# A new order, a third bank for the maxima and unread products for TensorE in a four-layer transformer kernel

## The reference: what is computed

```python
x = _layernorm(x + _L0_attn_ref(x, ...))   # causal attention with rotary positions, 16 heads of 16 features
x = _layernorm(x + _L0_ffn_ref(x, ...))    # 8 experts, each token goes to its best one; 256 -> 512 -> 256, gelu
x = _layernorm(x + _L1_attn_ref(x, ...))   # local attention (window 128) mixed with 64 pooled latent tokens
x = _layernorm(x + _L1_ffn_ref(x, ...))    # 8 experts, one per sequence; 256 -> 64 -> 256, relu
```

## Time and profile before

| | |
|---|---|
| Median of three runs | 1435.85 us |
| The profiled execution | 1435.74 us |
| its span, first to last instruction | 1433.9 us |
| mean granted TensorE clock | 0.943 of full speed |
| PE, DVE, ACT, POOL busy | 84%, 65%, 42%, 19% |

### The profile page before, as it was taken

The page is one execution under the profiler, slowest core; times in us unless marked ns, Lnnn a source line. Parts: engine busy times, 40 slices in busy tenths (PEclk is TensorE's granted clock), DMA queues, the critical chain, the costliest instruction groups (busy, mean ns, idle before and its releaser), DMA issues. The chain is left out here.

```text
span 1433.9 us, 32422 instructions
## 1 busy us (share of the span) xinstructions
PE 1202.5 (84%) x12418; PEld 768.0 (54%) x12469; DVE 932.6 (65%) x2335; ACT 602.6 (42%) x1144; POOL 277.0 (19%) x294
## 2 busy tenths in 40 slices
PE   7579888889898889964999855999899999989854
PEld 3144545545454545543999733665656565555532
DVE  3676666666666666722777676777767677676732
ACT  1034444444444444532555312545455454545331
POOL 3111121111111120011111141213232322212022
PEclk9689999999999999996999978999999999999975
DMA  5341714141414131353422143451514334140000
GB/s 183 110 115 45 175 53 126 53 127 45 127 45 116 48 97 49 94 184 102 161 75 68 34 121 104 123 129 40 127 55 120 86 84 123 44 127 11 9 16 15
DMA packets 68264, 127.86 MB, mean 89 GB/s; under 512 B 8320, under 2 KB 58128, under 8 KB 64656
## 3 DMA queue, kind: packets, MB, share of 16 engines
q1 hardware_dynamic: 65040, 117.38, 29.2%
q0 software_dynamic: 3072, 8.41, 1.8%
HBM read 84.31 MB, written 40.66 MB: 87 GB/s over the span
## 5 line engine op out<-in xcount | busy, mean ns | idle before, releaser
L627 DVE TENSOR_REDUCE first_maxima<-bank 128x1 f32<-128x512 f32 (+3 forms) x352 | 220.6, 638 | 168.5 <-PE bank L397 167.2
L548 ACT ACTIVATE arena<-pair 128x512 f32<-128x512 f32 x320 | 187.3, 597 | 293.5 <-PE pair L426 291.5
L1473 ACT ACTIVATE second_probs<-pair 128x512 f32<-128x512 f32 (+1 forms) x256 | 135.3, 541 | 196.1 <-PE pair L1342 158.7
L394 PE MATMUL bank<-stacks 96*128 96x256 bf16 (+3 forms) x512 | 130.5, 312 | 39.5 <-DVE first_maxima L627 37.7
L1633 DVE TENSOR_REDUCE second_maxima<-bank 128x3 f32<-128x480 f32 (+1 forms) x160 | 105.2, 660 | 59.4 <-PE bank L1309 57.3
L373 PE MATMUL bank<-first_xT,w_qkv 128*128 128x512 f32 x256 | 129.7, 638 | 13.0 <-DMA first_xT<-in_xT 7.9
L419 PE MATMUL pair<-stacks 128*128 128x128 bf16 (+3 forms) x461 | 104.0, 295 | 0.9 <-ACT arena L548 0.5
L394 PEld LDWEIGHTS bank<-stacks 96*128 96x128 bf16 x512 | 45.1, 100 | 89.0 <-DVE first_maxima L627 59.1
L769 POOL TENSOR_TENSOR first_halves<-first_halves 128x512 f32<-128x512 f32 x32 | 41.5, 1296 | 264.4 <-DVE first_halves L612 264.4
L397 PE MATMUL bank<-constants_bf 128*128 128x128 bf16 (+2 forms) x352 | 88.7, 252 | 0.0
L1334 PE MATMUL pair<-second_q_stack,second_k_stack 128*32 128x160 bf16 (+4 forms) x2048 | 83.5, 230 | 3.2 <-ACT second_probs L1473 3.0
(11 more groups left out here) (337 smaller groups left out, 2406.7 us busy)
## 6 DMA issues: line engine op xcount, KB each, us to landing
stacks<-parked SPq DMA_DIRECT2D x96, 256.0 KB, 5.0
parked<-first_parts SPq DMA_DIRECT2D x32, 384.0 KB, 2.8
second_q_stack<-parked SPq DMA_DIRECT2D x48, 256.0 KB, 5.2
second_k_stack<-parked SPq DMA_DIRECT2D x48, 256.0 KB, 8.2
parked<-second_parts SPq DMA_DIRECT2D x30, 384.0 KB, 2.6
expert_xs<-sorted_x SPq DMA_DIRECT2D x39, 128.5 KB, 2.1
sorted_y<-expert_ys SPq DMA_DIRECT2D x39, 128.0 KB, 1.7
first_xT<-in_xT SPq DMA_DIRECT2D x8, 512.0 KB, 4.2
```

Source lines behind the costliest of these rows:

```text
L394: pe.matmul(mx[n % 2][:, x * wide:(x + 1) * wide], q[0:ROWS, i * GH + hh, qt * P:(qt + 1) * P], k[0:ROWS, i * GH + hh, 0:wide], start=(x = ...
L548: act.activation(PT[:, s:s + len(heads), lo:lo + each], ex[n % 3][:, 0:len(heads) * each].rearrange("p (h q) -> p h q", h=len(heads)), ACT ...
L627: dve.tensor_reduce(nm[:, i, qt, heads[0]:heads[0] + len(heads)], mx[n % 2][:, 0:wide].rearrange("p (h k) -> p h k", h=len(heads)), AX.X, ...
L1473: act.activation(PT[:, s:s + len(heads), lo:lo + each], scores[:, :, 0:each], ACT.Exp, scale=SCALE).then_inc(lp["exps"], 1)
```

## The change

Three things are changed at once.

First, `schedule0` adds a correction from a table `SHIFTED` to the time of each item (items of the first two batches with a time of their own in `front0` keep that). The sorted list of layer 0 gets another order by it.

Second, the third bank of `ex` goes to `mx`: maxima have three banks, exponentials two. PE may write a `max` item when the item three before it is read, and an `exp` item when the one two before it is read.

Third, `keep_busy` issues bf16 products of 512 columns which nothing reads, into a bank of the maxima.

```diff
+def keep_busy(pe, m, bank, count):
+    for _ in range(count):
+        pe.matmul(bank[:, :], m["idb"][:, :], spread(m["mT0"][:, :], P, NT), start=True, stop=True)
+SHIFTED = {
+    "add": {0: -0.032, 1: -0.093}, "exp": {None: -0.088}, "hi": {0: -0.04, 1: -0.079, 2: 0.027, 3: -0.079},
+    "lo": {0: 0.197, 1: 0.34, 2: 0.033, 3: 0.228}, "logit": {None: 0.02}, "new": {0: -0.174, 1: -0.059},
+    "norm": {0: -0.02, 1: -0.024, 2: 0.006, 3: -0.055}, "o_in": {None: -0.049}, "park": {2: 0.277},
+    "qk": {(0, 0): 0.025, (0, 1): 0.025, (1, 0): 0.025, (1, 1): 0.025, (2, 0): 0.019, (2, 1): 0.08, (3, 0): -0.298, (3, 1): 0.025},
+    "rest": {0: 0.006, 1: 0.109, 2: 0.166, 3: 0.2}, "rope": {(0, 0): -0.084, (0, 1): -0.099, (1, 0): -0.07, (3, 1): -0.103},
+    "split": {None: 0.054}, "stats": {0: -0.063, 1: -0.067}, "sum": {0: -0.183, 1: -0.128, 2: -0.128, 3: -0.128},
+    "turn": {None: 0.078}, "turn_a": {0: 0.097, 1: 0.024}, "turn_o": {0: 0.024, 1: 0.013, 2: 0.014, 3: -0.024},
+    "turn_x": {1: 0.012}, "turned": {None: 0.006}, "v": {0: -0.023, 1: 0.069}, "v_in": {1: 0.029}, "values": {0: 0.037},
+    "x_in": {0: -0.079, 1: -0.063}, "xt": {None: 0.068},
+}
     def at(time, kind, b, i=0, j=0):
+        moved = SHIFTED.get(kind, {})
+        time += moved.get(None, moved.get((i, j) if kind in ("qk", "rope") else j if kind == "values" else i, 0))
-        mx, wk = m["ps"][0:2], m["ps"][2:4]
-        ex = [m["pair"][0][:, 0:S], m["pair"][0][:, S:2 * S], m["pair"][1][:, 0:S]]
+        mx, wk = m["ps"][0:2] + [m["pair"][1][:, 0:S]], m["ps"][2:4]
+        ex = [m["pair"][0][:, 0:S], m["pair"][0][:, S:2 * S]]
-                        if n >= 2:
-                            pe.wait_ge(lp["s_max"], n - 1)
+                        if n >= 3:
+                            pe.wait_ge(lp["s_max"], n - 2)
-                        if n >= 3:
-                            pe.wait_ge(lp["exps"], n - 2)
+                        if n >= 2:
+                            pe.wait_ge(lp["exps"], n - 1)
# layer 0, last batch: before turn_x 0, and behind rank
+                            pe.wait_ge(lp["s_max"], NMAX * NG * B)
+                            keep_busy(pe, m, mx[1], 10)
+                            keep_busy(pe, m, mx[1], 32)
# experts: before the first tile, and behind the last
+                keep_busy(pe, m, ps[1], 6)
+                keep_busy(pe, m, ps[1], 24)
# layer 1: before the list, and before v 2 of batch 0
+                keep_busy(pe, m, mx[1], 24)
+                            keep_busy(pe, m, mx[1], 28)
# layer 1, last batch: before turn_a 0 (behind a wait for all maxima), turn_z 0 and h
+                            keep_busy(pe, m, mx[1], 22)
+                            keep_busy(pe, m, mx[1], 16)
+                            keep_busy(pe, m, mx[1], 10)
```

More of the change, by code:

```diff
@@ L422, in _ @@
                         if len(tiles) == 2:
[L423 removed]
+                            o = ex[n % 2][:, 0:2 * P].rearrange("p (r c) -> p r c", c=P)
                         else:
[L425 removed]
+                            o = ex[n % 2][:, 0:lo].rearrange("p (r c) -> p r c", r=len(heads))[:, :, 0:P]
                         ins = pe.matmul(o, m["idb"][:, :], spread(m["mT0"][:, :], P, len(heads) * len(tiles)), start=False,
@@ L480, in _ @@
                     elif kind == "turn_x":
+                        if b == B - 1 and i == 0:
+                            pe.wait_ge(lp["s_max"], NMAX * NG * B)
+                            keep_busy(pe, m, mx[1], 10)
                         pe.wait_ge(lp["x_new"], 2 * (b + 1))
@@ L548, in _ @@
                         act.activation(PT[:, s:s + len(heads), lo:lo + each],
-                                       ex[n % 3][:, 0:len(heads) * each].rearrange("p (h q) -> p h q", h=len(heads)),
+                                       ex[n % 2][:, 0:len(heads) * each].rearrange("p (h q) -> p h q", h=len(heads)),
                                        ACT.Exp, scale=SCALE).then_inc(lp["exps"], 1)
@@ L1276, in _ @@
                     elif kind == "v":
+                        if b == 0 and i == 2:
+                            keep_busy(pe, m, mx[1], 28)
                         bank = claim("v", b, i)
@@ L1400, in _ @@
                     elif kind == "h":
+                        if b == B - 1:
+                            keep_busy(pe, m, mx[1], 10)
                         pe.wait_ge(lp["near"], b + 1)
```

8 lines of the change are left out of this document (4 added, 4 removed).

## The result

The changed kernel takes 1358.08 us (median of 4 runs, 1352.82 to 1363.16), the one before 1436.38 on the same chip (4 runs, 1433.95 to 1438.61): a ratio of 0.9455, 95% interval 0.9416 to 0.9494. I had forecast 1403 and a range of 1384 to 1428.

What follows compares the result with a forecast made beforehand. The prediction took PE to bound layer 0, with chains between engines at a lower PE clock elsewhere. From 1435.7 us it took 22.4 for layer 0 and 9.7 for the unread products, predicting 1403 us, range 1384 to 1428.

Steps and rivals of the forecast that it cites:

- the rival in which PE waits for ACT: Layer 0: two exponential banks stall PE behind ACT's other work; 43 us slower there, 1469 us in all; chance 0.12.
- DVE's reductions: Rival for layer 0: DVE bounds the runs of maxima and the third bank gives nothing; 1420 us; chance 0.26.
- the 1.6 for the `norm`: Layer 0: PE's wait for the fourth `norm` before `turn_a`, 1.6 us per period, of which 1.3 was to go.
- the 1.7 for ACT's copy: Layer 0: PE's waits for the bank held by ACT's copy of the transposed maxima; 1.4 of 1.7 us to go.
- the one-hot matrix: Layer 0: `rank` waits 1.0 us for short DVE instructions behind `logit`; 0.3 us per period was to go.
- the one in which the waits go nearly all: Rival: layer 0 gains 5.5 us per period, 35 in all, and the products 12; 1389 us; chance 0.15.
- the sum of layer 0: Gains less costs give 3.5 us per period over 6.4 periods, 22.4 us; ends -11.8 and +7.2 per period.
- The maxima at half, 1.5: Layer 0: the third bank takes away half of PE's 2.9 us of waits for the maxima per period.
- the claims behind `rope`: Layer 0: `turn_o` and `out` claim a bank from a `rope` whose `qk` ended shortly before; costs 0.4 us per period.
- The end's term: Last batch: unread products before `turn_a` and `h` keep PE's clock up; two thirds of 7.4 us taken, 5.0.
- The other terms: Unread products at layer 0's end 1.0, experts' front 0.7, experts' end and layer 1's front 2.5, third `v` 0.5 us.
- The rule on program order: Matmuls run in program order, so a cold block of 22 before `turn_a` would make the end 2.2 us later.

Runs made afterwards that it cites:

- e1_banks: Only the new banks (three for maxima, two for exponentials), with the old order and no unread products, against the kernel before: 1415.47 us, ratio 0.9875.
- e2_order: Only the new order, with the old banks and no unread products, against the kernel before: 1368.59 us, ratio 0.9544.
- q0_change: The whole change run again on another chip, against the kernel before there: 1377.05 us, ratio 0.9509.
- f2_exp: Old banks, no unread products, only the table's entries for `exp`, `values` and `o_in`, against the kernel before: 1414.75 us, ratio 0.9878.
- e3_both: New order and new banks without the unread products, against the kernel before: 1362.93 us, ratio 0.9513.
- p1_end: The changed kernel with unread products only in the last batch (22, 16 and 10): 1361.33 us, ratio 0.9494 to the kernel before.
- p2_rest: The changed kernel without the last batch's 22, 16 and 10 unread products, other blocks kept: 1365.33 us, ratio 0.9525 to the kernel before.
- e4_products: Only the unread products, with the old order and old banks, against the kernel before: 1431.82 us, ratio 0.9989.
- q1_tail: The changed kernel with unread products only in the last batch, filled more closely (33, 3, 23, 10, 14, 6): 1374.48 us, ratio 0.9494 to the kernel before.
- q2_filled: The changed kernel with the last batch filled more closely and the other blocks kept: 1373.80 us, ratio 0.9489 to the kernel before.

## Why the prediction was wrong

**What was right.** PE bounds layer 0 and no other engine took its place; the rival in which PE waits for ACT needed 5.6 us a period, and PE's waits for the exponentials' banks sum to 1.9 us from 90 to 570 us, over seven periods. DVE's reductions did not become the bound. The waits of the earlier trace rows that I named went, and went further than I said: the 1.6 for the `norm` and the 1.7 for ACT's copy wholly (I had taken 1.3 and 1.4), the one-hot matrix by 0.6 (0.3). For the 0.7 of the copy before `turn_x` the reason was another than mine: the exponentials' shift removes it, not the place of `turn`. The rival nearest to what came was the one in which the waits go nearly all, and even that had 5.5 a period where 10.6 came.

**The step that failed** is the sum of layer 0: "1.4 + 1.3 + 1.5 + 0.3 - 0.6 - 0.4 = 3.5 us per period, 6.4 x 3.5 = 22.4". It gave 22 us, and layer 0 gave 73: its period fell by 10.6 us and not by 3.5. Four things are in it:

- *The upper end was the sum of the named waits, and it is no upper end.* I had put "+7.2, all named waits gone". Idle time was 8.59, of which 7.8 went, and PE's busy time fell by 2.8 us on top of it (65.80 to 63.04), most of it holds within the listed durations. 10.6 us a period went. The part within busy time alone is 2.8 x 6.4 = 18 us that no term of mine held.
- *The maxima at half, 1.5.* The third bank alone took away all 2.9 (e1_banks), and the order alone all but 0.4 (the one wait left in e2_order's period). Reading 0.6 us of relief against single waits of up to 0.9 was too local; that the new order spreads the reductions, so that seldom two of them press, is my reading and was not tested by itself. The term is 2.9 in the rows, and with 0.16 us more at each of its seven waits some 4.0.
- *Costs that did not come.* Two banks of exponentials cost one wait of 1.1 us in the old order and none in the period of the new one, where the exponentials stand elsewhere, against my 0.6 (on the other chip it is 0.8 in a period of q0_change); nor did the claims behind `rope` cost 0.4. I had priced the moved exponentials as a cost of the banks only; f2_exp shows that moving them is worth 3.5 a period.
- *Nothing for the front.* "For the front (until 130 us) ... I take nothing: transfers and DVE end the waits there." The 57th reduction of the maxima starts at 131.8 us in before and at 120.1 in the change, so the front up to my 130 us gave 11.7; by the first `rank` it is 19.4. The rows before that `rank` hold 20.5 us of waits for the maxima, of which 13.6 are left in e3_both. I had not looked at that stretch's waits. DVE does end them, but how far PE may run ahead is set by the banks: the banks alone bring the first `rank` forward by 7.4 us (193.1), the order alone by 13.0 (187.5), both by 20.9 (179.7).

**The products**: 9.7 forecast, about 4 measured (p1_end against p2_rest 4.0, e3_both to the change 4.9 by medians of two chips, e4_products 2.0). The end's term was 5.0, and the distance from the last batch's `turn_a` to the last instruction became 3.5 us shorter (41.4 to 37.9); what is missing is mostly the first `out`, which stayed at 3.75 us behind a gap of 2.5 us. The other terms (1.0 + 0.7 + 2.5 + 0.5 = 4.7) gave nothing that can be measured (q1_tail against q2_filled 0.7 us, p2_rest at 0.9525 where e3_both, without products, has 0.9513). At the front of layer 1 the first `qk` still takes 3.75, as I had said would prove that step wrong:

```profile
758.72 1.26 PE L1245 MATMUL bank<-constants,second_x 128*128 128x128 f32 x8 [2.04 <-DMA second_x<-sorted_y,place_dense]
760.76 3.75 PE L1261 MATMUL pair<-second_xT,arena 128*128 128x512 f32 x4 [0.78 <-ACT second_xT L1465]
```

**The rule on program order.** The block of 22 ran at the higher clock (4.91 us) and held nothing back. The 10 before `h` ran at the lower one, 4.01 us, and `h` followed at once, 4.48 us behind `rl` where it had been 4.36 in before: held back by 0.1 us, and then 1.8 shorter. So the trace agrees with the rule of the Trainium skill that the prediction names, at a price that was no part of the miss.

**The sum again**, from the traces: front up to the first `rank` 19.4, seven further batches 53.9 (four periods of 9.8 to 10.6, then 6.9, 4.0 and 1.6), and 4.7 behind layer 0. Of these, 3.5 lie behind the last `turn_a`; but 2.8 lie in the batch before it (60.2 and 57.4 us), where the two executions had another granted clock, and which the change does not touch. That part is luck of the two profiles, and the rest of what lies behind layer 0 became 1.6 longer.

## What to carry to other kernels

The idle time of the engine that binds is a lower bound of what an order can give, not the upper one: where matmul durations overlap in a stream, take the distance from start to start for the same pair of instructions, held and not held, and multiply what the list of waits leaves out by the number of waits. Read the waits of the first batches by themselves, even if only "the transfer" seems to end them. Compare busy times of PE only between traces with the same number of matmul records. Products that only keep the clock up were worth something here where nothing but a chain was left to run, and a gap of 2.5 us behind them took part of that away.

## What the runs showed that I had not expected

- The change seems to be worth less on the other chip: 0.9509 and 70.3 us there, 0.9455 and 78.3 at first, though the two intervals just overlap. The kernel before is slower there too, 1447.33 against 1436.38. The trace of q0_change shows periods of 65.0 to 65.4 us from the second on, where the first chip had 63.8 to 64.6. PE's waits for the exponentials' banks come back, 4.5 and 2.5 us from 90 to 570 us in q0_change where the change's first trace had 0.9 and 1.0, though the activations take the same 596 ns. Two banks leave little room; what sets it off there I did not find.

```profile
PE pair L441 <- ACT arena L574: 4.5, 7, 0.8
PE pair L448 <- ACT arena L574: 2.5, 3, 1.9
```

- 2.54 us without work after 4.9 us of products at the full clock were followed by a `turn_a` still at the full clock and then an `out` at half of it (3.75 us), while gaps of 0.17 us were not (1.97).
- The three parts of an order of over fifty small shifts added up to within 0.5 us of 10.
